# The experts' layer of a decoder block as one stream of token tiles, with each sum over the experts as one reduction of 1024 columns on VectorE

## The chip, the cores and the metric

The program runs on one core of a Trainium2 chip. The metric is the time of one execution on the device, in microseconds (us). The number compared is the median of several runs. Beside the runs there is one execution under the hardware profiler, and all durations below come from it.

## The reference

The program is one decoder layer on a batch of 4 sequences of 1024 tokens with 512 channels. Its three parts follow one another, each closed by a residual sum and a layer norm: a gated self-attention, a masked cross-attention, and an experts' layer. The change touches only the third, which is this part of the reference (cut):

```
rw = _gating(hidden_states, sim_matrix, gates)            # [4, 1024, 16 experts]
q = einsum('bte,bted->btd', rw, einsum('btc,ecd->bted', hidden_states, q_proj))
k = einsum('bte,bted->btd', rw, einsum('btc,ecd->bted', hidden_states, k_proj))
v = einsum('bte,bted->btd', rw, einsum('btc,ecd->bted', hidden_states, v_proj))
scores = where(causal, einsum('bqd,bkd->bqk', q, k) * scale, -inf)
attn = einsum('bqk,bkd->bqd', softmax(scores), v)
mixed = attn[:, :, None, :] * rw[..., None]
return einsum('bted,edc->btc', mixed, o_proj)
```

`_gating` normalizes each token (a root of the sum of its squares), multiplies by a normalized matrix of 16 columns, subtracts a gate, falls back on the best two experts where none is positive, and takes a softmax over the active ones. Each of q, k and v is 16 projections of 64 columns, so 1024 columns for each token, weighted by `rw` and summed over the 16 experts down to 64.

## The kernel before, in words

`expert_layer` runs after the two attentions, as five instruction streams, one for each engine, joined by semaphores. Within a stream the order is fixed by the list `ffn_steps()`, and each engine walks this list in order. The loop around it runs over the 4 batches (`Fori(0, B)`).

A token tile is 128 tokens, so a batch has 8 tiles. Arrays that feed accurate products are kept as a high and a low half (`x`, `w_in`, `w_out`, `mixed_t`), and `parts` in TensorE's stream issues three matmuls for each of them: 12 matmuls of 512 columns for one projection step, 24 for one output step. All results go through a ring of eight PSUM banks (`work0` to `work7`); each step takes the next bank, waits on `work_free` of that bank, and its reader waits on `work_full`.

The order within a batch:

- The whole sequence `x` is loaded and split (ScalarE writes the high half, VectorE at L1897 the low half), GpSimd makes the squares, and TensorE makes the sums of squares and the logits of all 8 tiles (`SQ`, `LT`, `LG`).
- `LG` on VectorE is the routing of all 8 tiles at once: a chain of small instructions (L1903 to L1961) with two round trips to ScalarE, a square root (L1800) and an exponential (L1803).
- 48 steps `proj`: for each of six weight blocks `w` (two halves each of q, k and v) and each tile, TensorE makes 128x512, VectorE weights it (L1969) and sums its 8 experts (L1975). For the second half it adds the two half sums (L1978).
- `turn` turns q and k of all tiles, then 10 slots run the causal attention of the tiles, two tiles apart: in a slot TensorE does `mixed_t` of tile n-2, `prob_t` of tile n-1, `score` of tile n, `pv` of tile n-1 and `out` of tile n-2. VectorE finds the maxima (L1989 to L1997), makes `mixed` (L2011, L2014), the low half of `mixed_t` (L2022), and the residual sum and layer norm of `out` (L2031 to L2061). ScalarE does the exponentials (L1817) and the high half of `mixed_t` (L1832).
- One store of the whole batch. The next batch's `x` is loaded as soon as the projections are done.

The weights are loaded once ahead of the loop, 16 chunks through four staging buffers: ScalarE copies the high half of a chunk, VectorE subtracts (L1887).

Of the kernel before, what the change touches and what calls it, by code (L numbers as in the profile page):

```python
# [6 lines left out]
P = 128  # L7
B, S, D, H = 4, 1024, 512, 16
DH = D // H
KT = D // P  # L10
# [252 lines left out]
class Ring:  # L263

    def __init__(self, lists, kinds):

        self.count = Count(lists, lambda s: s[0] in kinds)
        assert self.count.body % 2 == 0

    def place(self, sec, step):  # L270

        c = self.count
        n = c.at[sec.number][step]
        if sec.number == 0:
            return n % 2, n // 2
        if sec.number == 1:
            return (c.first + n) % 2, sec.i * (c.body // 2) + (c.first + n) // 2
        n += c.first + (B - 1) * c.body
        return n % 2, n // 2
# [1139 lines left out]
SUM = 32  # L1419
WS, WK = 4, 2  # L1420
# [5 lines left out]
INV = HD ** -0.5  # L1426


def ffn_steps():

    steps = [("SQ", 0), ("SQ", 1), ("LT", 0), ("LT", 1), ("LG",)] + [("proj", w, t) for w in range(6) for t in range(TT)]
    steps += [("turn", n) for n in range(TT // 2)]
    halves = lambda qt: range(1 if qt < TT // 2 else 2)
    for n in range(TT + 2):
        if 2 <= n:
            steps += [("mixed_t", n - 2, g) for g in range(2)]
        if 1 <= n <= TT:  # L1440
            steps += [("prob_t", n - 1, c) for c in halves(n - 1)]
        if n < TT:
            steps += [("score", n, c) for c in halves(n)]
        if 1 <= n <= TT:
            steps.append(("pv", n - 1))
        if 2 <= n:
            steps.append(("out", n - 2))
    while len(steps) % RING:
        steps.append(("pad", len(steps) % RING))
    return steps  # L1450


def expert_layer(nc, io):

    steps = ffn_steps()
    PER = len(steps) // RING
    use_no = {s: n for n, s in enumerate(steps)}  # L1460
    ctx = ExitStack()
    with ctx:
# [5 lines left out]
        def sb(name, shape, dt=F32, at=None):  # L1468
            n = 4
            for k in shape[1:]:  # L1470
                n *= k
            if at is None:
                at = start + used[0]
                used[0] += -(-n // 64) * 64
                assert used[0] + 64 <= size, (name, used[0], size)
            place[name] = at
            return nc.alloc_sbuf_tensor_at(f"{name}_e", shape, dt, offset=at)

        place = {}
# [4 lines left out]
        x = sb("x", [P, 2, KT, S], F32R)  # L1484

        prob = sb("prob", [P, 2, S], at=place["x"])
        mixed_t = sb("mixed_t", [P, 2, FK, P], F32R, at=place["x"] + 8 * S)
        prob_t = sb("prob_t", [P, TT, P])
        y = sb("y", [P, TT, D])
        w_stage = sb("w_stage", [P, WS, WK, CH], at=place["y"])  # L1490
        weighted = sb("weighted", [P, 2, CH])
        mixed = sb("mixed", [P, E, HD], at=place["weighted"])

        lg_t = sb("lg_t", [SUM + 1, S], at=place["weighted"])
        part = sb("part", [P, HD])
        qkv = sb("qkv", [P, 3, TT, HD])
        q_t = sb("q_t", [HD, S])
        k_t = sb("k_t", [HD, S])
# [3 lines left out]
        squares = sb("squares", [P, 2, S], at=place["q_t"])  # L1502
        sim_raw = sb("sim_raw", [P, KT, E])
        sim_sq = sb("sim_sq", [P, KT, E])
        sim = sb("sim", [P, 2, KT, SUM], F32R)
# [3 lines left out]
        lg = sb("lg", [P, TT, E])  # L1509
        rw = sb("rw", [P, TT, E])  # L1510
        pick = sb("pick", [P, TT, E])

        beats = sb("beats", [P, TT, E, E], at=place["q_t"])
        small = sb("small", [P, 10, TT])
        nmax = sb("nmax", [P, TT, 2])
        total = sb("total", [P, TT, 2])
        rtot = sb("rtot", [P, TT])
        attn = sb("attn", [P, HD])
# [18 lines left out]
        x_over = sem("x_over")  # L1537
        x_raw = sem("x_raw")
        x_hi = sem("x_hi")
        squared = sem("squared")  # L1540
        squares_used = sem("squares_used")
        scores_done = sem("scores_done")
        lt_ready = sem("lt_ready")
        x_ready = sem("x_ready")
        proj_done = sem("proj_done")
        res_in = sem("res_in")
        routing_in = sem("routing_in")
        routing_out = sem("routing_out")
        qkv_ready = sem("qkv_ready")
# [8 lines left out]
        sd_ready = sem("sd_ready")  # L1558
# [3 lines left out]

        w_chunks = [w_in[:, w, :, k:k + WK, :] for w in range(6) for k in range(0, KT, WK)]
        w_chunks += [w_out[:, :, k:k + WK, :] for k in range(0, FK, WK)]
        NW = len(w_chunks)
        halves = lambda qt: range(1 if qt < TT // 2 else 2)

        keys = lambda qt, c: min(CH, (qt + 1) * P - c * CH)

        scored = lambda qt: sum(len(halves(q)) for q in range(qt + 1))  # L1570
        SC = scored(TT - 1)

        def turned_logits(bank):
            return bank[:, 0:TT * (SUM + 1)].rearrange("p (t e) -> p t e", t=TT)

        def wait_full(eng, i, step):

            n = use_no[step]
            eng.wait_ge(work_full[n % RING], i * PER + n // RING + 1)
            return bank_of[n % RING], work_free[n % RING]  # L1580
# [8 lines left out]
        def _(sp):  # L1589
            for t, src in ((eye, io["eye"]), (causal, io["causal"])):  # L1590
                sp.dma_start(t[:, :], src).then_inc(const_in, 16)
# [542 lines left out]
```

## Time and profile before

| what | value |
|---|---|
| median of 3 runs | 4721.47 us (4720.66 to 4730.45) |
| profiled execution | 4720.34 us, with a span of 4718.5 us from its first to its last instruction |
| granted TensorE clock, mean over the span | 0.943 |
| TensorE (PE) busy | 4197.2 us, 89% |
| VectorE (DVE) busy | 2688.8 us, 57% |
| ScalarE (ACT) busy | 1609.3 us, 34% |
| GpSimd (POOL) busy | 1397.8 us, 30% |

The time of the profiled execution is its span and 1.8 us around it. "Busy" is an average over all three parts of the layer. The experts' layer is the last part of the span, and the rows below all lie in it. A position such as 4107.24 is in microseconds from the start of the span. The granted clock is a share of 2.4 GHz, so 1.00 is the upper level of TensorE's clock and 0.50 the lower, 1.2 GHz.

### The profile page before, as it was taken

What the parts mean: (1) busy time and instruction counts of PE and PEld (TensorE: products, weight loads), DVE (VectorE), ACT (ScalarE), POOL (GpSimd) and SP (SyncE); (2) the same over time, 40 slices, a digit from 0 to 9 for tenths busy, and PEclk for the clock granted to TensorE, in tenths of its full rate; (3) what the DMA queues carried; (4) which work ended last, traced back from release to release, by engine and by line L of the source; (5) the groups of instructions that cost most, each with busy time, mean ns of one, the idle gap of its engine ahead of it and who ended that gap; (6) DMA issues with size and microseconds to landing.
All of it is one profiled execution on the core that took longest, in us unless ns stands there. A gap on an engine that the chain in (4) does not pass through costs nothing. (4 is left out here: it accounts for less than half of the span.)

```text
span 4718.5 us, 62570 instructions
## 1 busy us (share of the span) xinstructions
PE 4197.2 (89%) x21356; PEld 2425.0 (51%) x21356; DVE 2688.8 (57%) x3648; ACT 1609.3 (34%) x2897; POOL 1397.8 (30%) x800
## 2 busy tenths in 40 slices
PE   5899899989999984899989989998996699999997
PEld 3443643554364433543644364446443476767686
DVE  2564465446445633575567466745773766667585
ACT  1354254335524541244234424432443212020202
POOL 1223222312322221376257535752662000000000
PEclk8999899989999997899989999999998899999898
DMA  2221322142123205212422241234111301010100
GB/s 85 65 63 51 83 61 52 48 104 50 45 68 90 48 21 175 63 41 73 133 65 58 90 127 40 68 99 112 41 28 51 112 19 37 18 37 18 37 1 18
DMA packets 120954, 294.62 MB, mean 62 GB/s; under 512 B 18544, under 2 KB 20464, under 8 KB 120624
## 3 DMA queue, kind: packets, MB, share of 16 engines
q1 hardware_dynamic: 110128, 273.06, 21.3%
q10 hardware_dynamic: 10496, 17.31, 1.0%
q8 instruction: 189, 3.10, 0.3%
q14 instruction: 141, 1.16, 0.1%
HBM read 145.87 MB, written 43.25 MB: 40 GB/s over the span
## 5 line engine op out<-in xcount | busy, mean ns | idle before, releaser
L1100 ACT ACTIVATE probs<-half 128x512 f32<-128x512 f32 x2048 | 1112.8, 595 | 1017.3 <-PE half L904 468.1
L901 PE MATMUL half<-stack 97*128 97x512 f32 x2048 | 877.5, 492 | 65.3 <-ACT probs L1100 27.9
L1331 DVE TENSOR_REDUCE mx<-wide 128x1 f32<-128x1024 f32 x512 | 601.8, 1220 | 560.5 <-PE wide L862 554.3
L1327 DVE CUSTOM_DVE_ANT_0 wide<-wide,mask_q 128x1024 f32<-128x1024 f32 x512 | 617.5, 1247 | 280.4 <-PE wide L862 262.8
L862 PE MATMUL wide<-stack 96*128 96x512 f32 x2048 | 652.2, 434 | 90.5 <-DVE mx L1331 39.2
L901 PEld LDWEIGHTS half<-stack 97*128 97x128 f32 x2048 | 374.8, 194 | 679.5 <-ACT probs L1100 318.2
L766 POOL TENSOR_TENSOR psums<-psums,probs 128x1024 f32<-128x1024 f32 x232 | 550.1, 2391 | 158.8 <-ACT probs L1100 139.5
L845 PE MATMUL acc<-probs,v 128*32 128x512 f32 x4096 | 554.5, 612 | 3.1 <-ACT u L1069 3.0
L1675 PE MATMUL work_e<-w_in_e,x_e 128*128 128x512 f32 x2304 | 524.0, 389 | 0.0
L862 PEld LDWEIGHTS wide<-stack 96*128 96x128 f32 x2048 | 389.0, 197 | 214.8 <-DVE mx L1327 66.2
L1675 PEld LDWEIGHTS work_e<-w_in_e,x_e 128*128 128x128 f32 x2304 | 431.9, 188 | 90.6 <-DVE weighted_e L1969 1.0
L904 PE MATMUL half<-mask_k,eye 128*128 128x512 fp8e5 x1024 | 406.8, 397 | 0.0
L845 PE MATMUL acc<-probs,e_one 128*2 128x512 f32 x2048 | 274.9, 604 | 0.0
L1657 POOL TENSOR_TENSOR squares_e<-x_e 128x1024 f32<-128x1024 f32 x16 | 35.1, 2203 | 802.4 <-PEq L1762 642.1
L804 PE MATMUL half<-wkv,stack 128*128 128x512 f32 x768 | 188.7, 404 | 56.0 <-POOLq L707 46.4
L804 PE MATMUL half<-w,ct 128*128 128x512 f32 x768 | 187.4, 406 | 47.1 <-POOLq L788 47.1
L1675 PE MATMUL work_e<-w_out_e,mixed_t_e 128*128 128x512 f32 x768 | 205.8, 429 | 16.7 <-DVEq L2024 16.7
L904 PEld LDWEIGHTS half<-mask_k,eye 128*128 128x128 fp8e5 x1024 | 100.5, 98 | 227.8 <-issue 198.2
L804 PE MATMUL half<-stack,wkv 128*128 128x512 f32 x768 | 188.6, 404 | 23.6 <-POOLq L707 20.4
L804 PEld LDWEIGHTS half<-wkv,stack 128*128 128x128 f32 x768 | 147.0, 194 | 96.8 <-issue 50.6
L804 PEld LDWEIGHTS half<-w,ct 128*128 128x128 f32 x768 | 150.1, 197 | 84.8 <-issue 46.4
L804 PE MATMUL half<-stack,w 128*128 128x512 f32 x768 | 185.1, 395 | 4.5 <-DVEq L1252 3.0
(247 smaller groups left out, 4381.3 us busy)
## 6 DMA issues: line engine op xcount, KB each, us to landing
stack<-qk SPq DMA_DIRECT2D x336, 256.0 KB, 4.9
y<-x SPq DMA_DIRECT2D x8, 2048.0 KB, 8.5
x<-y SPq DMA_DIRECT2D x8, 2048.0 KB, 7.8
x_t<-xts ACTq DMA_DIRECT2D x16, 1024.0 KB, 5.6
mstage<-mask SPq DMA_DIRECT2D x32, 512.0 KB, 4.1
mstage<-mask_t SPq DMA_DIRECT2D x32, 512.0 KB, 3.9
stage<-x_t SPq DMA_DIRECT2D x24, 512.0 KB, 3.6
stack<-first SPq DMA_DIRECT2D x48, 256.0 KB, 5.0
```

Source lines behind the costliest of these rows:

```text
L766: op = lambda h: pool.tensor_tensor(psums[:, h, :], psums[:, h, :], probs[:, kt % 2 * 2 + h, :], ALU.add)
L804: last = pe.matmul(out, a(k), b(k), start=(k == 0 and n == 0), stop=(k == KT - 1 and n == 2))
L845: last = pe.matmul(out, left, right[:, c * CH:(c + 1) * CH], start=opens or ((kt == 0) and not (masked and part)), stop=closes or ((kt == ...
L862: last = pe.matmul(bank[:, c * CH:(c + 1) * CH], stack[0:3 * DH, SLOT[p], h, t * P:(t + 1) * P], stack[0:3 * DH, SLOT[p], 2 + h, c * CH:(c ...
L901: last = pe.matmul(bank[:, :], stack[0:3 * DH + 1, s, 2 + h, kt * P:(kt + 1) * P], stack[0:3 * DH + 1, s, h, c * CH:(c + 1) * CH], start=T ...
L904: last = pe.matmul(bank[:, :], eye8[:, :], mask_k[:, kt, c * CH:(c + 1) * CH], start=False, stop=True)
L1100: act.activation(probs[:, kt % 2 * 2 + h, c * CH:(c + 1) * CH], bank[:, :], ACT.Exp, scale=SCALE).then_inc(free, 1)
L1327: dve.tensor_tensor_reduce(bank[:, :], bank[:, :], mask_q[:, t, :], 1.0, -3e38, ALU.add, ALU.max, mx[:, p % 3, n:n + 1]).then_inc(free, 1)
L1331: dve.tensor_reduce(mx[:, p % 3, n:n + 1], bank[:, :], AX.X, ALU.max).then_inc(free, 1)
L1657: pool.tensor_tensor(squares[:, k % 2, :], raw, raw, ALU.mult).then_inc(squared, 1)
L1675: last = pe.matmul(out, a(k), b(k), start=(k == 0 and n == 0), stop=(k == tiles - 1 and n == 2))
```

## The change

The experts' layer no longer goes through its phases batch by batch. `token_sections()` makes one stream of the 32 tiles: a slot `token_slot(g, tile)` holds the projections of tile `now`, the attention of the tile before it (`one`), the output and layer norm of the tile before that (`two`), and the load, the split, the logits and the routing of the tiles that follow (`nxt`, `after`). An opening list holds the first two slots and the weight chunks, a loop body of eight slots runs three times, and a closing list holds eight slots and ends with the last tiles. Projections of a tile are now all six blocks in a row (`p` 0 to 5), not one block over all tiles.

Further edits with it:

- `weighted` holds both halves, 1024 columns, and one reduction over the 16 experts (new L1970) takes the place of two reductions of 512 columns and an addition.
- The routing runs once for each tile on 128x16 tiles, 24 instructions, with the exponential's round trip inside it. The sum of squares is one ScalarE instruction with accumulation (new L1798), its root new L1803.
- The low half of `x` (new L1664) and the scaling of the layer norm (new L1670) move from VectorE to GpSimd.
- `mixed` is one instruction instead of two (new L2003).
- The root of the variance (new L1808) and the five small instructions that refine it (new L2032 to L2040) run once for each tile.
- The weights have two staging buffers instead of four.
- Tiles are loaded and stored one by one.
- ScalarE's stream has a semaphore increment, `alone(act)`, between a wait and the activation behind it at nearly every step.

```diff
-def ffn_steps():
-    steps = [("SQ", 0), ("SQ", 1), ("LT", 0), ("LT", 1), ("LG",)] + [("proj", w, t) for w in range(6) for t in range(TT)]
...
+def token_slot(g, tile):
+
+    two, one, now, nxt, after = (tile(n) for n in range(g - 2, g + 3))
+    keys = key_halves(one[1]) if one else ()
+    order = [
+        ("load", after), ("split", nxt), ("square", nxt),
+        ("p", now, 0), ("turn", one), ("out", two), ("p", now, 1),
+        *[("score", one, c) for c in keys],
+        ("lg", nxt), ("norm_root", nxt), ("var_root", two), ("p", now, 2), ("ln", two), ("p", now, 3),
+        *[("prob_t", one, c) for c in keys],
+        ("route", nxt), ("p", now, 4), ("pv", one), ("store", two), ("p", now, 5), ("mixed_t", one, 0), ("mixed_t", one, 1),
+    ]
+    return [step for step in order if step[1]]
...
+    for step in token_slot(0, opening) + token_slot(1, opening):
+        if step[0] == "p" and step[1] == (1, 0) and step[2]:
+            first += [("w", 2 * step[2]), ("w", 2 * step[2] + 1)]
+        if step[0] == "p" and step[1] == (1, 1) and step[2] < 4:
+            first.append(("w", 12 + step[2]))
+        first.append(step)
...
 VectorE
-                        prod = weighted[:, t % 2, :]
+                        prod = weighted[:, (3 * t + w // 2) % 2, w % 2 * CH:(w % 2 + 1) * CH]
...
-                        dve.tensor_reduce(target, prod.rearrange("p (e d) -> p d e", d=HD), AX.X, ALU.add)
                         if w % 2:
-                            dve.drain()
-                            dve.tensor_tensor(qkv[:, w // 2, t, :], qkv[:, w // 2, t, :], part[:, :], ALU.add)
+                            dve.drain().then_inc(weighted_in, 1)
+                            both = weighted[:, (3 * t + w // 2) % 2, :].rearrange("p (e d) -> p d e", d=HD)
+                            dve.tensor_reduce(qk[:, t % 2, w // 2, :] if w < 4 else v[:, t, :], both, AX.X, ALU.add)
+                            dve.drain().then_inc(summed, 1)
...
 ScalarE
+                    elif kind == "norm_root":
+                        act.wait_ge(squared, number + 1)
+                        alone(act)
+                        act.activation(root[:, t:t + 1], sums[:, t:t + 1], ACT.Sqrt)
+                        act.drain().then_inc(rooted, 1)
+                    elif kind == "route":
+                        act.wait_ge(pick_in, number + 1)
+                        alone(act)
+                        act.activation(pick[:, :], pick[:, :], ACT.Exp)
+                        act.drain().then_inc(pick_out, 1)
```

The first place is TensorE's stream between two output steps. Before, in a slot of the attention of a batch (L1734 is `prob_t`, L1728 `score`, L1740 `pv`, and L1675 with `w_out` is `out`):

```order
L1747 MATMUL work_e<-eye_e,mixed_e 128x128 [waits mixed_ready_e,work_free2_e]
L1747 MATMUL work_e<-eye_e,mixed_e 128x128 x3
L1734 MATMUL work_e<-eye_e,prob_e 128x128 [waits prob_ready_e]
L1728 MATMUL work_e<-k_t_e,q_t_e 128x512 [waits work_free4_e]
L1740 MATMUL work_e<-qkv_e,prob_t_e 128x64 [waits prob_t_ready_e]
L1675 MATMUL work_e<-w_out_e,mixed_t_e 128x512 [waits lo_ready_e]
L1675 MATMUL work_e<-w_out_e,mixed_t_e 128x512 x23
```

After the change, from `pv` of a slot over its end into the next slot (L1740 is `pv`, L1746 `mixed_t`, L1723 `turn`, L1692 is a projection with `w_in` and `out` with `w_out`):

```order
L1740 MATMUL work_e<-v_e,prob_t_e 128x64 x2
L1692 MATMUL work_e<-w_in_e,x_e 128x512 [waits work_free6_e]
L1692 MATMUL work_e<-w_in_e,x_e 128x512 x11
L1746 MATMUL work_e<-eye_e,mixed_e 128x128 [waits work_free7_e,mixed_ready_e]
L1746 MATMUL work_e<-eye_e,mixed_e 128x128 [waits work_free0_e,mixed_ready_e]
L1692 MATMUL work_e<-w_in_e,x_e 128x512 [waits work_free1_e]
L1692 MATMUL work_e<-w_in_e,x_e 128x512 x11
L1723 MATMUL work_e<-eye_e,qk_e 64x128 [waits summed_e]
L1692 MATMUL work_e<-w_out_e,mixed_t_e 128x512 [waits lo_ready_e]
L1692 MATMUL work_e<-w_out_e,mixed_t_e 128x512 x23
L1692 MATMUL work_e<-w_in_e,x_e 128x512 [waits work_free4_e]
```

The transposes of `mixed`, which wait for `mixed_ready`, now stand ahead of the next tile's first projection, and `out` of the same tile stands right behind that projection.

The second place is VectorE's stream in a slot after the change, from the sum of k to the low half of `mixed_t`. L1937 is the last of the 24 instructions of the routing of the next tile, L1963 the weighting of a projection, L2003 makes `mixed`:

```order
L1970 TENSOR_REDUCE qk_e<-weighted_e 128x64
L1866 TENSOR_SCALAR root_e<-root_e 128x1 [waits rooted_e]
L1920 TENSOR_SCALAR pick_e<-lg_e,small_e 128x16
L1931 TENSOR_TENSOR rw_e<-rw_e,pick_e 128x16 [waits pick_out_e]
L1937 TENSOR_SCALAR rw_e<-rw_e,small_e 128x16
L1963 TENSOR_TENSOR weighted_e<-work_e,rw_e 128x512 [waits work_full2_e]
L1997 TENSOR_TENSOR rtot_e<-total_e 128x1 [waits prob_ready_e]
L2003 SCALAR_TENSOR_TENSOR mixed_e<-work_e,rtot_e,rw_e 128x1024
L1963 TENSOR_TENSOR weighted_e<-work_e,rw_e 128x512 [waits work_full4_e]
L1970 TENSOR_REDUCE v_e<-weighted_e 128x64
L2014 TENSOR_TENSOR mixed_t_e<-work_e,mixed_t_e 128x512 [waits hi_ready_e]
```

The whole routing of tile `nxt` stands ahead of `mixed` of tile `one`. Before, the routing of a whole batch was over before the first of its projections was weighted.

The third place is ScalarE's stream. Before, in the routing of a batch:

```order
L1800 ACT_TABLE_LOAD
L1800 ACTIVATE small_e<-small_e 128x8 [waits routing_in_e]
L1803 ACT_TABLE_LOAD
L1803 ACTIVATE pick_e<-pick_e 128x128 [waits routing_in_e]
L1808 ACTIVATE q_t_e<-work_e 64x256 [waits work_full5_e]
```

After, in a slot (L1827 is the exponential of the scores, L1803 the root for the token's norm, L1808 the root of the variance):

```order
L1827 ACTIVATE prob_e,total_e<-work_e,nmax_e 128x512 [waits masked_in_e,work_full3_e]
L1827 ACTIVATE prob_e,total_e<-work_e,nmax_e 128x256 [waits masked_in_e,work_full4_e]
L1803 ACT_TABLE_LOAD [waits squared_e]
L1803 ACTIVATE root_e<-sums_e 128x1
L1808 ACTIVATE sd_e<-tmp_e 128x1 [waits var_ready_e]
```

The load of a function table stood ahead of the wait and now stands behind it. A slot has two such loads, this one and one for the exponential of the routing, which waits for `pick_in` in the same way.

## Rows read from the trace of the kernel before

**Rows 1.** Span and granted clock of the core.

```profile
core 0: 4718.5 us, clock 0.943
```

**Rows 2.** Chain that ended last, the projections: start, us, what.

```profile
3715.99 130.92 PE work_e L1675 x576
...
4474.97 130.94 PE work_e L1675 x576
```

**Rows 3.** Windows: weights, then one batch's attention; busy us of each engine, PEclk, DMA.

```profile
3661.00:3703.00 42.00, 10.74 (x24) 3.38 (x24) 27.38 (x30) 18.89 (x20) 10.42 (x4) 0.62 0.75 255
3864.00:3946.00 82.00, 75.05 (x376) 59.38 (x376) 46.43 (x97) 24.14 (x48) 3.75 (x2) 0.96 0.00 1
```

**Rows 4.** Timeline of the projections: start, us, engine, line, [idle before].

```profile
4049.82 11.95 PE L1675 MATMUL work_e<-w_in_e,x_e 128*128 128x512 f32 x52
...
4058.18 0.69 DVE L1969 TENSOR_TENSOR weighted_e<-work_e,rw_e 128x512 f32<-128x512 f32 x1 [0.87 <-PE work_e L1675]
4058.97 1.07 DVE L1975 TENSOR_REDUCE qkv_e<-weighted_e 128x64 f32<-128x512 f32 x1
```

**Rows 5.** Groups by line, experts' layer: busy us, mean ns, idle before.

```profile
L1975 DVE TENSOR_REDUCE qkv_e<-weighted_e 128x64 f32<-128x512 f32 x96 | 102.7, 1070 | 8.8
...
L2014 DVE TENSOR_TENSOR mixed_e<-attn_e,rw_e 128x1024 f32<-128x1024 f32 x32 | 39.2, 1225 | 4.4 <-issue 1.8
...
L1817 ACT ACTIVATE prob_e<-work_e,nmax_e 128x512 f32<-128x512 f32 (+3 forms) x48 | 27.9, 582 | 75.0 <-DVEq L1998 72.3 <-issue 2.7
...
L1991 DVE TENSOR_REDUCE nmax_e<-work_e 128x1 f32<-128x512 f32 (+3 forms) x48 | 26.8, 558 | 5.5 <-issue 2.5
...
L1817 ACT ACTIVATION_READ_ACCUMULATOR prob_e<-work_e,nmax_e 128x1 f32 x48 | 9.2, 192 | 0.0
L1926 DVE TENSOR_REDUCE rw_e<-beats_e 128x128 f32<-128x2048 f32 x4 | 9.1, 2286 | 0.3
```

**Rows 6.** Timeline of a slot in the attention of a batch.

```profile
4135.01 5.74 PE L1675 MATMUL work_e<-w_out_e,mixed_t_e 128*128 128x512 f32 x24
...
4140.59 1.04 PE L1747 MATMUL work_e<-eye_e,mixed_e 128*128 128x128 f32 x8
...
4140.79 0.69 DVE L2031 TENSOR_TENSOR y_e<-work_e,y_e 128x512 f32<-128x512 f32 x1 [2.02 <-PE work_e L1675]
...
4142.46 0.69 DVE L2022 TENSOR_TENSOR mixed_t_e<-work_e,mixed_t_e 128x512 fp32r<-128x512 f32 x1
...
4143.36 0.69 DVE L2022 TENSOR_TENSOR mixed_t_e<-work_e,mixed_t_e 128x512 fp32r<-128x512 f32 x1 [0.21 <-issue]
```

**Rows 7.** Timeline of the routing of a batch, VectorE and ScalarE.

```profile
3964.65 1.28 ACT L1800 ACT_TABLE_LOAD   x1 [0.17 <-issue]
...
3965.94 0.21 ACT L1800 ACTIVATE small_e<-small_e 128x8 f32<-128x8 f32 x1
3966.30 1.28 ACT L1803 ACT_TABLE_LOAD   x1
3966.32 0.17 DVE L1862 TENSOR_SCALAR small_e<-small_e 128x8 f32<-128x8 f32 x1 [0.81 <-ACTq L1801]
...
3967.86 0.29 DVE L1910 TENSOR_TENSOR lg_e<-work_e,small_e 128x128 f32<-128x128 f32 x1
...
3983.51 0.28 DVE L1948 TENSOR_TENSOR pick_e<-lg_e,small_e 128x128 f32<-128x128 f32 x1
3983.85 0.31 ACT L1803 ACTIVATE pick_e<-pick_e 128x128 f32<-128x128 f32 x1 [16.27 <-DVEq L1949]
```

**Rows 8.** Windows of TensorE: us, busy (instructions), granted clock.

```profile
4441.00:4442.00 1.00, 0.00 (x0) 1.00 0.00 0
...
4443.00:4444.00 1.00, 0.00 (x0) 0.66 0.00 0
4444.00:4445.00 1.00, 0.85 (x2) 0.50 0.00 0
...
4450.00:4451.00 1.00, 1.00 (x6) 0.93 0.00 0
```

More of the change, by code:

```diff
@@ L1426 @@
 INV = HD ** -0.5
-def ffn_steps():
-    steps = [("SQ", 0), ("SQ", 1), ("LT", 0), ("LT", 1), ("LG",)] + [("proj", w, t) for w in range(6) for t in range(TT)]
[L1435 to L1450, printed above, removed]
+BANK_KINDS = ("lg", "p", "turn", "out", "score", "prob_t", "pv", "mixed_t", "pad")
@@ new lines, in token_sections @@
+def token_sections():
+    opening = lambda n: (1, n) if n >= 0 else None
+    inner = lambda n: (n // TT, n % TT)
+    closing = lambda n: (0, n) if n < TT else None
+    first = [("load", (1, 0)), ("w", 0), ("w", 1), ("load", (1, 1)), ("split", (1, 0)), ("square", (1, 0)),
+             ("lg", (1, 0)), ("norm_root", (1, 0)), ("route", (1, 0))]
+    for step in token_slot(0, opening) + token_slot(1, opening):
[4 more added lines that the diff above has]
+        first.append(step)
+    body = [step for g in range(2, TT + 2) for step in token_slot(g, inner)]
+    body += [("pad", n) for n in range(-sum(step[0] in BANK_KINDS for step in body) % RING)]
+    return first, body, [step for g in range(2, TT + 2) for step in token_slot(g, closing)]
@@ L1453, in expert_layer @@
 def expert_layer(nc, io):
-    steps = ffn_steps()
-    PER = len(steps) // RING
-    use_no = {s: n for n, s in enumerate(steps)}
+    lists = [list(steps) for steps in token_sections()]
+    ring = Ring(lists, BANK_KINDS, RING)
     ctx = ExitStack()
@@ new lines, in parts, with run @@
+            def parts(out, hi_l, lo_l, hi_r, lo_r, tiles=KT):
+                for k in range(tiles):
+                    for n, (a, b) in enumerate(((hi_l, hi_r), (hi_l, lo_r), (lo_l, hi_r))):
+                        last = pe.matmul(out, a(k), b(k), start=(k == 0 and n == 0),
+                                         stop=(k == tiles - 1 and n == 2))
+                return last
+            def run(sec):
+                for step in sec.steps:
+                    kind = step[0]
+                    if kind not in BANK_KINDS:
+                        continue
+                    b, n = ring.place(sec, step)
+                    bank = bank_of[b]
+                    if sec.number or n > 0:
+                        pe.wait_ge(work_free[b], n)
+                        alone(pe)
+                    tile = step[1]
+                    t = 0 if kind == "pad" else tile[1]
+                    number = None if kind == "pad" else token_tile(sec, tile)
+                    if kind == "lg":
+                        pe.wait_ge(x_ready, number + 1)
+                        last = parts(bank[:, 0:E], lambda k: x[:, t % 2, 0, k, :], lambda k: x[:, t % 2, 1, k, :],
+                                     lambda k: sim[:, 0, k, :], lambda k: sim[:, 1, k, :])
+                    elif kind == "p":
+                        w = step[2]
+                        if sec.number == 0 and t == 0:
@@ L1845, in _ @@
+                        bank, free = full(act, sec, step)
+                        alone(act)
+                        act.activation(mixed_t[:, 0, g * 4:g * 4 + 4, :].rearrange("p k n -> p (k n)"), bank[:, :], ACT.Copy)
+                        act.drain().then_inc(hi_ready, 1)
+            run(Section(0, None, False, True, lists[0]))
+            with act.Fori(0, B - 1) as i:
+                run(Section(1, i, True, True, lists[1]))
+            run(Section(2, None, True, False, lists[2]))
         @block.vector
```

725 lines of the change are left out of this document (334 added, 391 removed).

## The prediction

> **What bounds the kernel now.** I read the span and clock first [rows 1], then the chain of work that ended last. The change touches only what lies behind 3661, so the reader needs this stretch alone. The chain holds four blocks of 576 projection matmuls of 130.9 us, (4474.97 - 3715.99) / 3 = 253.0 us apart [rows 2]. So the layer is 42 us of weights [rows 3], some 13 us to the first projection, then 253 us a batch, ending at 4718.5. A batch is 131 us of projections and 122 us of the rest, that is 31.6 us a tile. In the projections TensorE issues a matmul every 11.95 / 52 = 0.23 us and never waits, so one `p` of 12 costs 2.73 us; VectorE, at 0.69 us for the weighting and 1.07 us for the sum, idles 0.87 us a step [rows 4]. In the attention stretch TensorE is busy 75 of 82 us [rows 3]. What a stream could win is the cover of the other 122 us; what it risks is that a tile's handovers between engines become the period.
>
> **The new slot, engine by engine.** TensorE: six `p` 16.4 us, `out` 5.7 and `mixed_t` 1.04 [rows 6], and estimates from the matmuls of such sizes for turn 0.3, scores 1.3, logits (12 narrow matmuls at 0.13 to 0.23 us) 2, `prob_t` and `pv` 1.6: 28 us.
>
> VectorE: six weightings, 0.79 us from start to start [rows 4]: 4.7. Three sums of 1024 columns, which the trace does not show. The sum of 512 costs 1070 ns, 2.09 ns a column; the reduction over adjacent columns costs 2286 ns for 2048, 1.12 ns a column [rows 5]. The old sum and the new one both step 64 columns between addends. If the surplus is per column, the new sum is two old ones less one fixed cost of about 0.15: 1.98 us; if it is per output (64 in both), it is about 1.6; at the adjacent rate it is 1.15. I take 1.98, since it doubles the nearest row, and keep 1.15 to 2.14. With 0.08 behind it: 2.06, so 6.2 for three. The edit by itself saves only one short addition and a fixed cost for each pair.
>
> The Trainium skill (VectorE: DVE Perf Modes, the perf-mode tier table) gives `tensor_reduce` the 1x mode whatever the operand, which would make 1024 columns some 1.2 us. By the page each sum costs 0.8 us less and the total below falls by about 47 us; the row of 512 columns, at 1.07 us where that rate gives about 0.7, speaks against it here.
>
> Routing: six small instructions take 3967.86 - 3966.32 = 1.54 us [rows 7], about 0.25 each. The 24 are six of these (1.5), one on PSUM (0.35), three of 256 columns at 0.42 and two reductions of 256 at 0.42 with 0.08 between (2.5), four small ones to `pick_in` (0.9): 5.2 us. Then the exponential's round trip. The root's row shows its parts: load 1.28, function 0.21, 0.17 until VectorE goes on [rows 7]. Before, the load of the exponential's table ran at 3966.30, long before its input came at 3983.8 [rows 7]; now it waits behind `pick_in`, so the trip is 1.9 us with 0.2 for waits. The last four cost 1.0. Sum 8.1 us a tile. Residual sum, statistics and two small ones 2.1, maxima 1.75 (1.5 of them a tile at 0.56 [rows 5], causal part and small ones), layer norm refinement 1.4, `mixed` 1.8 (1.23 on 1024 columns [rows 5], with the small ones before it), low halves 1.8 [rows 6]. VectorE: 28 us as well, wait for the exponential included.
>
> Both sums are below 31.6. The period is neither.
>
> **The period.** T = 0 is when `mixed` of a tile is ready. TensorE's next instructions in order are its transposes, then `p` 0 of the next tile, the turn, then `out` of the same tile: 0.15 + 1.04 + 2.73 + 0.3 = 4.2 us to the start of `out`. VectorE meanwhile does weighting 0.8, sum of v 2.06, low halves 1.8: 4.7. Then `out` takes 5.7: end at 10.4, and VectorE has idled 5 us, because all else it could do stands behind `out` in its list.
>
> From the end E of `out`, VectorE: residual and statistics lie under `p` 1 of TensorE (2.73), weighting of `p` 1 at E+3.6, sum of q E+5.7, maxima E+7.45. ScalarE: exponentials of the scores, 1.5 a tile at 0.58 + 0.19 [rows 5], E+8.7; then the square root's table, behind them, and both roots, 2.05: E+10.75. VectorE waits there (the weighting of `p` 2 is hidden): refinement E+12.15, weighting of `p` 3 E+12.95, sum of k E+15.0, routing E+23.1, weighting of `p` 4 E+23.9, `mixed` E+25.7. TensorE passes `p` 3 at E+11.5 and `p` 5 at E+18.6 or so, and then sits idle 7 us until `mixed` is ready. The eight banks don't help: what blocks it is `mixed_ready`, and `p` 0 of the next tile stands behind it.
>
> The clock: with TensorE idle from 4441 on, its clock fell to the lower level within the window from 4443, stayed there when dense work began behind 4444, and was back at about 4450 [rows 8]. An idle stretch of 7 us comes in every slot, so I let the first 6 us behind T = 0 run at the lower level: 2.9 us lost, `out` starts at 7.1 and E = 12.8. Bounds: no loss (E = 10.4) to 4.5 us (E = 14.4).
>
> Period 12.8 + 25.7 = **38.5 us** against 31.6.
>
> **The sum.** The opening: norm chain and two chunks 15 us as now, one routing 8, slot 0 some 46 us (its VectorE work 19, ten chunks of 1.3, and with only two staging buffers a load of about 4 us shows three times), slot 1 some 31: `mixed` of tile 0 at about 3661 + 101 = 3762. Then slots 2 to 31: 30 x 38.5 = 1155, to 4917. Closing: last `out` of tile 30, the scores, exponentials, `pv` and `out` of tile 31, its layer norm and store: 44. Span 4961, with 1.8 around it 4963 us. The profiled execution stands 1.1 us under the median, so against the median it is 4964: 5% slower. No change would need a period of (4718.5 - 3762 - 44) / 30 = 30.4 us. Work moved to GpSimd I cost at nothing: the low half of `x` has all of `mixed_t`, `p` 0, `out` and `p` 1, 15 us, before the logits read it, and the scaling of the layer norm feeds only a store; past 15 us it would delay the logits and through them the routing. Loads run two tiles ahead and cost nothing.
>
> **Rivals.**
> (1) The engines do overlap, and the slot is bound by its fullest engine: 28 to 28.5 us, so 3762 + 30 x 28.5 + 44 + 2 = 4663 us, faster. For it: both sums, and the ring of eight banks. Against: the transposes ahead of `p` 0 in TensorE's order. It decides if VectorE reaches `mixed` within 20 us behind E, that is if routing and sums cost less than 5 us instead of 12. 8%.
> (2) Slower, but less: the sum is cheap (1.15, which takes 1.7 off the path) and the clock stays up (2.4 off): 34.4 us, 4840 us. For it: the adjacent rate in rows 5. 14%.
> (3) Slower still: each wait with its semaphore increments costs 0.1 us more than counted, over some 15 waits, and the clock returns 1 us later: 41 us, 5038 us. 6%.
> (4) A table switch costs more than its load. Two stand on the path, and at 2.7 instead of 1.3 us each the period is 41.3, 5047 us. Against: in rows 7 the root starts 0.01 us behind its load, and the load 0.17 behind the engine's previous work. 2%. The Trainium skill (ScalarE: Activation LUTs, What ACT_TABLE_LOAD costs) states this price, load and drain together.
> (5) Gain and loss cancel within 0.2% (what a measurement of this kernel tells from no change): a period near 30.4. 2%.
> The forecast, period 36 to 40.5, has 68%. Slower is 68 + 14 + 6 + 2 = 90%, same 2%, faster 8%. The range leaves out (1), (5) and the outer end of (2) to (4): 4845 to 5045.
>
> **What would show it.** A period near 38 us in the experts' layer, TensorE idle about 7 us a slot ahead of the transposes of `mixed` and waiting for VectorE, its clock at 0.5 behind each such gap; VectorE idle 5 us or more ahead of the residual sum, waiting for `out`, and about 1 us ahead of L1931; the sum of 1024 columns at 1.98 us; two table loads a slot, each behind its wait; projections no longer one unbroken block. I am wrong if TensorE runs through a slot without that gap, if the sum takes about 1.2 us, or if the clock stays at 1.00.

## The result, and the profile after

The changed kernel takes 4960.44 us (median of 4 runs, 4958.61 to 4961.03) against 4721.07 us: ratio 1.0502, 95% interval 1.0484 to 1.052, 5% slower. The forecast was 4963 us for the profiled execution, which took 4959.92 us, and 4964 us for the median. The change touches only the experts' layer, so the rows below are of that part. "For [rows 1]" means that the rows are to be set beside that group.

Span and granted clock of the changed kernel, for [rows 1]:

```profile
core 0: 4958.1 us, clock 0.920
```

The chain of work that ended last (start, us, what), for [rows 2]. The blocks of 576 matmuls are gone. There is one piece of 36 in each slot, the 24 matmuls of `out` with the 12 of p1:

```profile
3783.15 8.20 PE work_e L1692 x36
...
4275.73 8.19 PE work_e L1692 x36
4315.29 8.19 PE work_e L1692 x36
4354.01 8.19 PE work_e L1692 x36
...
4885.22 8.20 PE work_e L1692 x36
```

The timeline of one slot (start, us, engine, line, [idle before]), for [rows 4, 6, 7]. The reader should follow VectorE from `mixed` (L2003) to the next L2003:

```profile
4307.28 1.28 DVE L2003 SCALAR_TENSOR_TENSOR mixed_e<-work_e,rtot_e,rw_e 128x1024 f32<-128x1024 f32 x1
4308.66 1.97 PE L1746 MATMUL work_e<-eye_e,mixed_e 128*128 128x128 f32 x8 [6.62 <-DVEq L2007]
4308.81 0.69 DVE L1963 TENSOR_TENSOR weighted_e<-work_e,rw_e 128x512 f32<-128x512 f32 x1 [0.25 <-issue]
4309.64 1.93 DVE L1970 TENSOR_REDUCE v_e<-weighted_e 128x64 f32<-128x1024 f32 x1
...
4310.29 4.79 PE L1692 MATMUL work_e<-w_in_e,x_e 128*128 128x512 f32 x12
...
4312.88 0.69 DVE L2014 TENSOR_TENSOR mixed_t_e<-work_e,mixed_t_e 128x512 fp32r<-128x512 f32 x1 [0.32 <-issue]
...
4315.05 5.70 PE L1692 MATMUL work_e<-w_out_e,mixed_t_e 128*128 128x512 f32 x24
...
4320.90 0.69 DVE L2020 TENSOR_TENSOR y_e<-work_e,y_e 128x512 f32<-128x512 f32 x1 [4.98 <-PE work_e L1692]
...
4333.29 0.16 DVE L2032 RECIPROCAL rstd_e<-sd_e 128x1 f32<-128x1 f32 x1 [2.79 <-ACTq L1809]
...
4337.54 3.01 PE L1692 MATMUL work_e<-w_in_e,x_e 128*128 128x512 f32 x12
4337.68 0.15 DVE L1866 TENSOR_SCALAR root_e<-root_e 128x1 f32<-128x1 f32 x1 [0.31 <-issue]
...
4344.66 0.17 DVE L1931 TENSOR_TENSOR rw_e<-rw_e,pick_e 128x16 f32<-128x16 f32 x1 [0.95 <-ACTq L1814]
...
4346.94 1.28 DVE L2003 SCALAR_TENSOR_TENSOR mixed_e<-work_e,rtot_e,rw_e 128x1024 f32<-128x1024 f32 x1
```

TensorE idles 6.6 us ahead of the transposes while VectorE routes and makes `mixed`, then VectorE idles 5.0 us while TensorE makes `out`. The groups (busy us, mean ns, idle before), for [rows 5], say the same for all 32 tiles:

```profile
L1970 DVE TENSOR_REDUCE qk_e<-weighted_e 128x64 f32<-128x1024 f32 x64 | 124.0, 1937 | 8.6
...
L1746 PE MATMUL work_e<-eye_e,mixed_e 128*128 128x128 f32 x256 | 62.1, 423 | 244.2 <-DVEq L2007 244.2
...
L2020 DVE TENSOR_TENSOR y_e<-work_e,y_e 128x512 f32<-128x512 f32 x32 | 22.1, 691 | 165.0 <-PE work_e L1692 165.0
L1931 DVE TENSOR_TENSOR rw_e<-rw_e,pick_e 128x16 f32<-128x16 f32 x32 | 5.6, 175 | 31.3 <-ACTq L1814 31.3
L2032 DVE RECIPROCAL rstd_e<-sd_e 128x1 f32<-128x1 f32 x32 | 5.2, 164 | 59.8 <-ACTq L1809 59.8
```

Windows of TensorE around the transposes at 4308.66 (busy, granted clock), for [rows 8]:

```profile
4306.00:4307.00 1.00, 0.00 (x0) 1.00 0.00 0
4307.00:4308.00 1.00, 0.00 (x0) 0.67 0.00 0
4308.00:4309.00 1.00, 0.34 (x2) 0.50 0.00 0
...
4313.00:4314.00 1.00, 1.00 (x4) 0.50 0.00 0
4314.00:4315.00 1.00, 1.00 (x6) 0.92 0.00 0
```

The clock falls to the lower level near the end of the idle stretch and is back about 5.5 us after work resumes; p0 takes 4.79 us. Over the first 30 slots, 2.8 to 8.4 us of the time from T, when `mixed` is ready, to the start of the residual sum are at the lower level, 4.9 us in the mean.

### The profile page after: what moved, and what is told of

It reads as the page before. It is cut to its first block and busy times, and to the rows that moved or that the text cites. A ratio compares the mean times of both kernels' runs of the same rounds, so it can differ in the third digit from the quotient of the medians.

```text
span 4958.1 us, 65804 instructions
## 1 busy us (share of the span) xinstructions
PE 4241.0 (86%) x21492; PEld 2483.5 (50%) x21492; DVE 2713.5 (55%) x4095; ACT 1700.0 (34%) x3116; POOL 1470.4 (30%) x848
## 5 line engine op out<-in xcount | busy, mean ns | idle before, releaser
L1692 PE MATMUL work_e<-w_in_e,x_e 128*128 128x512 f32 x2304 | 628.6, 429 | 36.5 <-DVEq L1949 32.3
L1692 PEld LDWEIGHTS work_e<-w_in_e,x_e 128*128 128x128 f32 x2304 | 471.7, 210 | 141.5 <-DVEq L1949 34.6
L1746 PE MATMUL work_e<-eye_e,mixed_e 128*128 128x128 f32 x256 | 62.1, 423 | 244.2 <-DVEq L2007 244.2
L1670 POOL TENSOR_SCALAR y_e<-y_e,mv_e,rstd_e 128x512 f32<-128x512 f32 x32 | 66.5, 2078 | 634.0 <-DVEq L2041 634.0
L1963 DVE TENSOR_TENSOR weighted_e<-work_e,rw_e 128x512 f32<-128x512 f32 x192 | 132.8, 691 | 152.3 <-PE work_e L1692 129.2
L1664 POOL TENSOR_TENSOR x_e<-x_raw_e,x_e 128x512 fp32r<-128x512 f32 x32 | 41.2, 1287 | 582.0 <-ACT x_e L1794 582.0
```

Of the source, the lines that this page charges most:

```text
L1692: last = pe.matmul(out, a(k), b(k), start=(k == 0 and n == 0), stop=(k == tiles - 1 and n == 2))
L1963: dve.tensor_tensor(prod.rearrange("p (e d) -> p e d", d=HD), bank[:, :].rearrange("p (e d) -> p e d", d=HD), rw[:, t, (w % 2) * 8:(w % 2) ...
```

## The experiments

All versions but one start from the changed kernel. The ratios are against the kernel before on the same chip (1.0502 for the changed kernel); "a slot" is the mean distance of the starts of `mixed` over the first 30 slots. This table, which I worked out from the timelines, splits the slot as the prediction did. T is when `mixed` is ready (0.1 us behind the end of its instruction), E the start of the residual sum. The columns are means over the 29 slots that hold a routing, and so a little longer than the mean slot.

| us | T to `out` | T to E | E to `ln` | E to routing of the changed order | E to next T | a slot |
|---|---|---|---|---|---|---|
| predicted | 7.1 | 12.8 | 10.75 | 15.0 | 25.7 | 38.5 |
| changed kernel | 6.18 | 12.04 | 10.94 | 15.40 | 25.95 | 37.76 |
| matmuls in the gap | 5.63 | 11.52 | 10.94 | 15.40 | 25.96 | 37.23 |
| roots early | 5.86 | 11.74 | 9.42 | 14.66 | 24.33 | 35.83 |
| two short sums | 6.15 | 12.02 | 10.46 | 14.28 | 26.13 | 37.86 |
| experts adjacent | 6.07 | 11.95 | 10.62 | 14.74 | 25.58 | 37.26 |
| routing late | 5.53 | 12.34 | 10.49 | moved | 19.38 | 31.67 |
| both | 5.51 | 12.49 | 8.23 | moved | 17.14 | 29.59 |
| both, split later | 5.58 | 11.74 | 8.62 | moved | 17.53 | 29.25 |

**Routing late.**

```diff
-        ("route", nxt), ("p", now, 4), ("pv", one), ..., ("mixed_t", one, 1),
+        ("p", now, 4), ("pv", one), ..., ("mixed_t", one, 1), ("route", nxt),
...
-        ... ("ln", two), ("p", now, 3),
+        ... ("ln", two), ("route_in", nxt), ("p", now, 3),
```

> Edit, on the changed kernel: the routing of the next tile is cut in two; its first seven instructions, which free the bank of the logits, stand behind `ln`, and the rest (some 7 us of small instructions on VectorE) stands behind the last subtraction of `mixed_t`, where VectorE otherwise waits for `out` and p1. Same work, another order. Theory (the routing on VectorE between k's sum and p4 is on the path, while 5 us of wait stand ahead of `out`): the slot falls by 7 us, and the pause of TensorE with it, and with that some of the half clock: 30 to 32 us a slot, 4720 to 4770 us. Rival (the sums of 1024 columns, or VectorE as a whole, are what binds): less than 60 us gained. Rival (the routing now delays p0's weighting and so frees its bank late, so `out` and p1 wait): 4850 to 4920.

Measured 4769.72 us, ratio 1.0112 (1.0088 to 1.0135). The slot fell by 6.1 us to 31.67, 184 of the 237 us by the ratios. Its timeline shows the routing where VectorE used to wait, and the transposes 2.5 us behind p5 instead of 6.6:

```profile
4177.40 1.09 PE L1747 MATMUL work_e<-eye_e,mixed_e 128*128 128x128 f32 x8 [2.54 <-DVEq L2013]
...
4182.49 5.74 PE L1693 MATMUL work_e<-w_out_e,mixed_t_e 128*128 128x512 f32 x24 [1.01 <-DVEq L2022]
4182.52 0.42 DVE L1909 TENSOR_TENSOR beats_e<-lg_e 128x256 f32<-128x256 f32 x1
...
4188.44 0.23 DVE L1941 TENSOR_SCALAR rw_e<-rw_e,small_e 128x16 f32<-128x16 f32 x1
4188.86 0.69 DVE L1969 TENSOR_TENSOR weighted_e<-work_e,rw_e 128x512 f32<-128x512 f32 x1 [0.19 <-issue]
4189.47 0.68 DVE L2026 TENSOR_TENSOR y_e<-work_e,y_e 128x512 f32<-128x512 f32 x1
```

The same instructions in another order took back most of the loss, so it is the place of the routing on one chain that costs, not its work. Some of the gain is the clock's: it now stays up from T to E in 17 of the 30 slots, and `out` starts 0.65 us earlier. VectorE, which had waited 5 us for `out`, now starts the residual sum 1.1 us behind its end instead of 0.15, which is why T to E rose by 0.3 all the same.

**Matmuls in the gap.** They are made to keep the clock up, and their results are used nowhere.

```diff
+                        if g == 0:
+                            for _ in range(24):
+                                pe.matmul(bank[:, :], w_in[:, 0, 0, 0, 0:P], w_in[:, 0, 0, 0, :], start=True, stop=True)
                         pe.wait_ge(mixed_ready, number + 1)
```

> Edit, on the changed kernel: before TensorE waits for `mixed` at the head of a slot it makes 24 more matmuls of 512 columns into the bank that the transposes of `mixed_t` then overwrite; their results are used nowhere, the output is as before. The wait of 7 to 8 us is then filled to about 5.5 us. Theory (the stretch at half clock behind the wait costs 2.9 us a slot, on the path): the clock stays at 1.00 through `mixed_t`, p0 and `out`, E falls by 2 to 2.9 us, 30 slots give back 60 to 87 us: 4875 to 4900 us. Rival (VectorE's own side, v's sum and the two subtractions, holds `out` back in any case, so the clock is off the path): within 25 us of 4960. Rival (the added matmuls are in the way): slower.

Measured 4943.37 us, ratio 1.0476 (1.0458 to 1.0495). The slot fell by 0.53 us only. In 12 of the 30 slots the clock stayed at 1.00 and p0 took 3.01 us:

```profile
4301.39 1.09 PE L1749 MATMUL work_e<-eye_e,mixed_e 128*128 128x128 f32 x8 [1.15 <-DVEq L2010]
...
4302.24 3.01 PE L1692 MATMUL work_e<-w_in_e,x_e 128*128 128x512 f32 x12
4302.36 2.00 DVE L1973 TENSOR_REDUCE v_e<-weighted_e 128x64 f32<-128x1024 f32 x1
...
4305.68 0.69 DVE L2017 TENSOR_TENSOR mixed_t_e<-work_e,mixed_t_e 128x512 fp32r<-128x512 f32 x1 [0.32 <-issue]
...
4306.48 5.73 PE L1692 MATMUL work_e<-w_out_e,mixed_t_e 128*128 128x512 f32 x24 [1.01 <-DVEq L2019]
```

With p0 short, `out` waits 1.0 us for VectorE's low halves, which end 5.0 us behind T. The sum of v stands ahead of them. In the other 18 slots the clock still fell around T, for 3.2 us or more before E, and p0 took 3.7 to 5.5 us. In the next slot, with T at 4339.80 (the timeline, then a window of TensorE with its granted clock, 0.50):

```profile
4340.65 4.59 PE L1692 MATMUL work_e<-w_in_e,x_e 128*128 128x512 f32 x12
...
4342.00:4343.00 1.00, 1.00 (x4) 0.50 0.00 0
```

So the edit kept the clock up only in part, and its 0.5 us is not the clock's whole price. The slots of the two traces give that. Two of the 30 are left out, in which p0 starts 2.3 to 3 us late at a turn of the loop in both versions (T at 4384.3 in the changed kernel is one). T to E is then 11.85 us in the changed kernel, 11.28 with the added matmuls, and 11.02 in the 12 slots with the clock up. The clock costs about 0.8 us a slot, not 2.9, and the edit took back 0.6 of it. The rival is borne out for the larger part: VectorE's own side holds `out` back until 5.1 us behind T, whatever the clock does.

**The roots early.**

```diff
-        ("load", after), ("split", nxt), ("square", nxt),
-        ("p", now, 0), ("turn", one), ("out", two), ("p", now, 1),
+        ("load", after), ("split", nxt), ("square", nxt), ("norm_root", nxt),
+        ("p", now, 0), ("turn", one), ("out", two), ("var_root", two), ("warm", ...), ("p", now, 1),
```

> Edit, on the changed kernel: on ScalarE the root of the next tile's norm stands right behind its square, the root of the variance right behind the copies of `turn`, and an exponential of one column whose result is used nowhere stands behind it, so that both table loads of a slot (1.28 us each) lie where ScalarE has nothing to do. Theory (VectorE waits 1.9 us for the root at `ln` and 1.0 us for the exponential in the routing, both on the path): 2.5 to 3 us a slot less, 75 to 95 us: 4865 to 4885 us. Rival (the waits only move to the bank of p3 or p4): within 20 us of 4960. Rival (the root now stands ahead of the exponentials of the scores and holds them back, since it waits for the sum of `out`): within 30 us, or slower.

Measured 4900.74 us, ratio 1.0387 (1.0369 to 1.0405), some 54 us less than the changed kernel by the ratios and 1.9 a slot, where I had expected 2.5 to 3. Both waits are nearly gone:

```profile
L1934 DVE TENSOR_TENSOR rw_e<-rw_e,pick_e 128x16 f32<-128x16 f32 x32 | 5.6, 176 | 4.0 <-ACTq L1817 0.9 <-issue 0.9
L2035 DVE RECIPROCAL rstd_e<-sd_e 128x1 f32<-128x1 f32 x32 | 4.9, 154 | 2.0 <-ACTq L1810 1.8 <-issue 0.2
```

That is 31.3 - 4.0 + 59.8 - 2.0 = 85 us of waits removed. VectorE's waits for TensorE at the weightings rose from 129.2 to 159.4 us. At `ln` 1.5 us were won, and 0.7 of them were still there at the routing: p3 was not ready any earlier. At the exponential, where nothing else is waited for, the whole 0.9 us counted.

**Two short sums for the wide one**, the edit of the title undone alone.

```diff
                         if w % 2:
-                            dve.tensor_reduce(... both, AX.X, ALU.add)
+                            dve.tensor_reduce(part, half, AX.X, ALU.add)
+                            dve.drain()
+                            dve.tensor_tensor(target, held, part, ALU.add)
+                        else:
+                            dve.tensor_reduce(held, half, AX.X, ALU.add)
```

> Edit, on the changed kernel: the sum of 1024 columns is undone alone: each weighted half is summed by an instruction of 512 columns as it comes, into two spare tiles of 64 columns, and an addition puts them together. One pair is then 2 x 1.07 + about 0.2 us instead of 1.94 us. Theory (the order of the stream sets the time, and the form of the sum hardly any): q's first half is summed in the wait for p1 and k's first half in the wait at `ln`, which takes 0.7 us each off the path, v's first half stands ahead of `mixed` and costs 0.3 us in the balance: 4925 us, between 4900 and 4970. Rival (the wide sum is what makes the changed kernel slow): a gain of 100 us or more. Rival (the wide sum is a gain as such): slower by 20 us or more.

Measured 4965.12 us, ratio 1.0523 (1.0505 to 1.0542), which can't be told from the changed kernel. The table has both sides. Up to the routing 1.1 us are won, of the 1.4 expected. Behind it they are lost again (E to T grows by 0.2 in all), since v's first half now stands ahead of `mixed` with its full 1.07 us, and nothing comes back behind it: `out` waits for TensorE's slow p0 there.

**The wide sum in the kernel before.**

```diff
-[("proj", w, t) for w in range(6) for t in range(TT)]
+[("proj", 2 * pair + half, t) for pair in range(3) for t in range(TT) for half in range(2)]
...
-                        dve.tensor_reduce(target, prod.rearrange("p (e d) -> p d e", d=HD), AX.X, ALU.add)
...
+                            both = weighted[:, :, :].rearrange("p h (e d) -> p d (h e)", d=HD)
+                            dve.tensor_reduce(qkv[:, w // 2, t, :], both, AX.X, ALU.add)
```

> Edit, on the kernel before: the sum alone is changed. Its stages stay, the projections are taken in pairs of halves for each tile, and each pair is summed by one instruction of 1024 columns. Theory (in this stage TensorE is busy without a pause and VectorE waits 0.9 us at each projection, so a shorter sum buys wait): within 15 us of the kernel before. Rival (the wide sum blocks banks for longer and stops TensorE, or by itself explains the loss of the changed kernel): slower by 50 us or more. Rival (the sum was on the path): faster by 3 x 0.4 us x 32 tiles, 38 us.

Measured 4723.08 us, ratio 1.0011 (0.9999 to 1.0023): nothing that can be told. The sum takes 1.98 us here and VectorE still waits for TensorE, for [rows 4]:

```profile
4061.32 0.69 DVE L1969 TENSOR_TENSOR weighted_e<-work_e,rw_e 128x512 f32<-128x512 f32 x1 [1.91 <-PE work_e L1675]
4062.10 1.98 DVE L1976 TENSOR_REDUCE qkv_e<-weighted_e 128x64 f32<-128x1024 f32 x1
```

So the exchange of the sums alone makes no difference that can be told, in either kernel, and the 5% are of the rest of the change.

**The experts adjacent in `weighted`.**

```diff
-                        prod = weighted[:, (3 * t + w // 2) % 2, w % 2 * CH:(w % 2 + 1) * CH]
+                        turn_ = weighted[:, (3 * t + w // 2) % 2, :].rearrange("p (d e) -> p e d", e=E)
...
-                            both = weighted[:, (3 * t + w // 2) % 2, :].rearrange("p (e d) -> p d e", d=HD)
+                            both = weighted[:, (3 * t + w // 2) % 2, :].rearrange("p (d e) -> p d e", e=E)
```

> Edit, on the changed kernel: the weighting writes its products with the 16 experts of one column next to each other (a step of 16 elements on the write), so that the sum over the experts reads neighbours instead of a step of 64 elements. Theory (the sum's 1.94 us is the price of its stepped reading; a reduction of 1024 neighbouring columns takes 1.22 us in the attention layers of this kernel): the sum takes 1.2 us, three sums a slot on the path give 2.1 us, 60 us in all, 4895 us, if the weighting stays at 0.69 us. Rival (the step costs the same on the write): the weighting rises to about 1.0 us, six a slot, and the time is within 25 us of the changed kernel. Rival (the step costs nothing either way, 1.9 ns a column is what an addition over 16 costs): no change in the sum, within 10 us.

Measured 4943.66 us, ratio 1.047 (1.0446 to 1.0494), 0.5 us a slot less than the changed kernel. The instructions of `weighted` (min/median/max ns):

```profile
L1963 DVE TENSOR_TENSOR weighted_e<-work_e,rw_e x192: 1011/1024/1069, 3694.3 to 4900.3; 128x512 f32<-128x512 f32 x192
L1970 DVE TENSOR_REDUCE qk_e<-weighted_e x64: 1219/1220/1223, 3704.6 to 4895.9; 128x64 f32<-128x1024 f32 x64
```

Stepped reading made the sum 1.94 us; with neighbours it is 1.22. The step is paid on the write instead, 0.33 us a weighting, as the first rival had it. A pair costs the same in all, and only what stands behind its second half is 0.4 us shorter.

**Both orders at once**, routing late and roots early, the edits of the two diffs above.

> Edit, on the changed kernel: the routing moved behind `mixed_t` and the roots moved ahead of the exponentials, both at once. Theory (each takes its own piece of one chain, so the gains add; the late routing gave 31.7 us a slot, the tables another 1.9 to 2.7 us): 29.0 to 29.8 us a slot, 4685 to 4710 us, faster than the kernel before. Rival (with the routing gone the wait at `ln` lies beside TensorE's own chain, which ends no earlier than VectorE): 31 us or more a slot, 4750 us.

Measured 4710.33 us (12 runs), ratio 0.998 (0.9968 to 0.9991), 29.59 us a slot. The gains add (6.1 and 1.9 us apart, 8.2 together), and the stream is now 0.2% faster than the kernel before, by an interval that just leaves out 1.

**The short sums in that version**, with the edit of the two short sums.

> Edit: the version with routing late and roots early, but with each pair summed by two instructions of 512 columns and an addition. Theory (here VectorE has few waits left, so the longer work of the two short sums, 2 x 1.07 + 0.2 + two more fences against 1.94 us, three times a tile, is no longer hidden): 0.7 to 1.3 us a slot more than the same version with the wide sum, 20 to 40 us. Rival (the first halves still hide in waits, as in the changed kernel, where the exchange made no difference): within 10 us of it.

Measured 4746.7 us, ratio 1.0057 (1.0038 to 1.0076), 36 us more than with the wide sum, 1.2 us a slot. Where VectorE seldom waits, the wide sum is worth what its time says.

**A tensor_scalar that stands still.** In the version with both, GpSimd's low half of `x` and the routing's last instruction meet:

```profile
4074.91 1.29 POOL L1666 TENSOR_TENSOR x_e<-x_raw_e,x_e 128x512 fp32r<-128x512 f32 x1 [15.12 <-ACT x_e L1796]
4075.12 1.12 DVE L1944 TENSOR_SCALAR rw_e<-rw_e,small_e 128x16 f32<-128x16 f32 x1
```

16 columns take 1.12 us and end with GpSimd's instruction; elsewhere they take 0.23. Two further versions change this meeting.

```diff
-                dve.tensor_scalar(weight, weight, small[:, 6:7], None, ALU.mult)
+                dve.tensor_tensor(weight, weight, small[:, 6:7].to_broadcast([P, E]), ALU.mult)
```

> Edit: the version with routing late and roots early, with the last instruction of the routing (weights times the reciprocal of their sum, 128x16) as a tensor_tensor with the reciprocal spread, in place of a tensor_scalar. In that version this tensor_scalar takes 1.12 to 1.20 us where GpSimd's subtraction for the split of x is under way, ending within 0.05 us of it, and 0.23 us where it is not. Theory (a form of instruction that takes both of VectorE's port pairs is shut out by GpSimd, and tensor_tensor is no such form): the instruction takes 0.18 us everywhere and the time falls by about 0.9 us in some 25 slots, 20 to 25 us, 4685 to 4690 us. Rival (a tensor_tensor with both inputs in SBUF is shut out by a GpSimd instruction that reads SBUF, as the Trainium skill has it, SBUF - State Buffer): it takes 1.1 us again, and the time is within 8 us of the version it comes from, 4710 us.

Measured 4705.0 us, ratio 0.9976 (0.9964 to 0.9988), 29.59 us a slot as before it. The other form is shut out just so:

```profile
4075.54 1.29 POOL L1666 TENSOR_TENSOR x_e<-x_raw_e,x_e 128x512 fp32r<-128x512 f32 x1 [15.09 <-ACT x_e L1796]
4075.74 1.12 DVE L1944 TENSOR_TENSOR rw_e<-rw_e,small_e 128x16 f32<-128x16 f32 x1
```

My theory fell and the rival holds. The Trainium skill (SBUF — State Buffer, Who interferes with whom) says that a VectorE instruction with two SBUF inputs contends with a GpSimd instruction that reads SBUF. This trace agrees, 1.12 us for 0.17.

```diff
-        ("load", after), ("split", nxt), ("square", nxt), ("norm_root", nxt),
-        ("p", now, 0), ("turn", one), ("out", two),
+        ("load", after),
+        ("p", now, 0), ("turn", one), ("split", nxt), ("square", nxt), ("norm_root", nxt), ("out", two),
```

> Edit: the version with routing late and roots early, with ScalarE's split and square of x behind the copies of `turn` instead of ahead of them, so that GpSimd's subtraction starts some 0.5 us later, behind the last instruction of the routing. Theory (that instruction's 0.9 us of standing still is on the path): it takes 0.23 us, the slot falls from 29.6 to about 28.8 us, 4685 to 4695 us. Rival (the next tensor_scalar or two-input instruction on VectorE is caught instead): within 8 us of 4710. Rival (VectorE then only waits for TensorE, which has 28 us of its own work a tile): 4700 to 4705.

Measured 4699.14 us, ratio 0.9969 (0.9956 to 0.9982), 29.25 us a slot. The instruction is back at 0.23 us and GpSimd starts behind it:

```profile
4070.81 0.23 DVE L1944 TENSOR_SCALAR rw_e<-rw_e,small_e 128x16 f32<-128x16 f32 x1
4071.24 1.29 POOL L1666 TENSOR_TENSOR x_e<-x_raw_e,x_e 128x512 fp32r<-128x512 f32 x1 [15.74 <-ACT x_e L1796]
```

T to E fell by 0.75 us, and E to T grew by 0.39: half of the gain is lost there. It goes into waits at the weightings. In the window 3765 to 4640 they rose by 13 us, those for TensorE by 21, in the version with both and in this one:

```profile
L1972 DVE TENSOR_TENSOR weighted_e<-work_e,rw_e 128x512 f32<-128x512 f32 x177 | 122.5, 692 | 74.8 <-issue 38.6 <-PE work_e L1694 36.3
L1972 DVE TENSOR_TENSOR weighted_e<-work_e,rw_e 128x512 f32<-128x512 f32 x180 | 124.5, 691 | 88.0 <-PE work_e L1694 57.3 <-issue 30.7
```

TensorE is busy 837 of 877 us between the first and the 31st `mixed` here. The slot fell by 0.3 us, not by the 0.8 of my theory, and the time lies between the theory's 4685 to 4695 and the 4700 to 4705 of the rival in which VectorE only waits for TensorE. From the version with `tensor_tensor` on the same chip it is 6 us, and the intervals overlap.

**The experts adjacent in that version**, with the edit of the adjacent experts.

> Edit: the version before it in this list, and besides the experts of one column next to each other in `weighted`, so that a weighting takes 1.02 us (0.69 before) and a sum 1.22 us (1.94 before). A pair is then 3.26 us of VectorE's work instead of 3.32, so only the part behind the second half is shorter, by 0.39 us. Theory (VectorE is nearly always busy here, so the totals decide): within 8 us of that version. Rival (the time behind a second half decides, as in the changed kernel, where the exchange took 0.5 us off a slot): 12 to 20 us less.

Measured 4694.88 us, ratio 0.9961 (0.9948 to 0.9973), 29.26 us a slot: within 8 us, as the totals have it. It is the lowest time of the study, 0.4% below the kernel before.

## Why the prediction was right

**The period.** Predicted 38.5, measured 37.76. The mechanism is the predicted one: a handover chain through `mixed`, `out` and the routing, TensorE idle 244.2 / 32 = 7.6 us a tile (7 predicted), VectorE idle 165.0 / 32 = 5.2 ahead of the residual sum (5) and 1.0 us ahead of L1931 (1). E to T was 25.95 against 25.7. Moving the routing off the chain gave 6.1 us a slot.

**The clock was the mis-sized term.** I had 6 us at the lower level and 2.9 us lost by them, all on the path. The lower level lasts 4.9 us in the mean, and p0 ends 6.0 us behind T in the changed kernel against 3.9 with the clock up (the two slots at the turns of the loop left out), so TensorE's side loses 2.2 us. Of these 1.3 are hidden. I had VectorE's own side done 4.7 us behind T, and with the clock up it needs 5.0 to the end of the low halves and 5.1 to the start of `out`; the two sides overlap, and only what TensorE's slow side exceeds is paid, some 0.8 us. Without the loss E would have been 11.0, not my lower bound of 10.4.

**The sum of 1024 columns** was predicted at 1.98 us and took 1.94. The Trainium skill (VectorE: DVE Perf Modes, the perf-mode tier table) gives the reduction the 1x mode whatever the operand, by which I had estimated about 1.2 us. The traces agree where the 1024 columns are neighbours (1.22) and not with the step of 64. In the form with 512 columns the price is 1.04 to 1.07, so the surplus goes by columns.

**Tables.** 1.28 us a load and nothing behind it that could be seen: in this slot the load of L1813 runs from 4342.93 and VectorE goes on at 4344.66, 1.73 us for load, function and wait. Rival (4) is out. The Trainium skill (ScalarE: Activation LUTs, What ACT_TABLE_LOAD costs) gives 2.66 us for a switch, load and drain together. This trace does not agree, with 1.28 us for the load and the function 0.01 us behind it.

**The ends.** `mixed` of tile 0 was ready at 3776.7, not 3762, and the closing took 48.7 us, not 44. The period's error (30 x 0.74 = 22 us less) met 15 and 5 us more here, so that the total came out within 3 us is luck: errors that cancel. The period alone, 2% off, is what the working got right. In the opening TensorE waits for weights 32.3 us in five waits, and what it does between them runs at the lower clock, which I had not counted:

```profile
3693.79 5.49 PE L1692 MATMUL work_e<-w_in_e,x_e 128*128 128x512 f32 x12 [7.31 <-DVEq L1949]
...
3732.24 5.36 PE L1692 MATMUL work_e<-w_in_e,x_e 128*128 128x512 f32 x12 [14.05 <-DVEq L1949]
```

The first five projections take 4.5 to 5.5 us instead of 2.73, 12 us more in all. Whether these make up the 15 us was not tried, nor were four staging buffers.

**GpSimd at nothing** held in the changed kernel: its two instructions take 1.29 and 2.08 us, far inside the 15 us of cover, and the logits never wait for them. In the version with both orders it did not, since VectorE stood still beside the first of them.

**Rival (1)** had the right bound for another order. With routing and roots moved, the slot is 29.6 us, and 29.25 with the later split, against its 28 to 28.5. It named the condition, `mixed` within 20 us behind E: moving the routing gave 19.4, and both moves 17.1, where TensorE's total begins to be felt. That TensorE's total limits it there was not tested by a run of its own; the growing waits for TensorE speak for it. The break-even period was predicted at 30.4 us; with the measured opening and closing it is (4718.5 - 3776.7 - 48.7) / 30 = 29.8. Only the versions with both moves and the wide sum are below it; with the short sums the slot is 30.8 us, and that version is 0.6% slower than the kernel before.

## What to carry to other kernels

In a stream where each engine walks one list, the period is the loop through the handovers, not the fullest engine; write it down from one result to the same result of the next tile, and look for long work on it that could stand where its engine waits. A shorter instruction pays only where its engine does not wait next: the same exchange of sums was worth nothing in two orders and 36 us in a third. When two sides race to one start, taking one side's delay away yields only the difference to the other. And a version that is made to take a delay away may do it in some slots only: here the clock stayed up in 12 of 30.

## What the runs showed that I had not expected

- A VectorE instruction of 16 columns stood still for 0.9 us beside a GpSimd subtraction, in both forms, `tensor_scalar` and `tensor_tensor` with two SBUF inputs. Instructions with one input in PSUM kept their time: the residual sum lay beside it in the version with the later split and took 0.68 us. So did the reduction: in the slot of the changed kernel k's sum (1.93 us from 4335.44) lay beside GpSimd's scaling of the layer norm (2.08 us from 4334.63).
- In these traces the step of an array costs VectorE on either side: 0.72 us on reading 1024 columns in steps of 64, and 0.33 us on writing 512 in steps of 16.
